# A convolution-style attention block and a token attention with top-2 experts on one core: a third of the copies into the query/key stacks moved from SyncE's queue to ScalarE's

## The reference

```
x   = x + proj(attention(group_norm(x)))            # conv block: 8 heads of 32, no mask
t   = tokens(x)                                      # 1024 tokens of 256
t   = t + W_O(causal_attention(layer_norm(t)))       # 8 heads of 32, causal
t   = t + experts(layer_norm(t))                     # 32 experts of 64, the 2 best by sigmoid gate
```

## Time and profile before

| | us |
|---|---|
| median of 3 runs | 3707.65 |
| the 3 runs | 3701.99 to 3708.15 |
| the profiled execution | 3706.1 |
| its span, first to last instruction | 3704.2 |
| PE busy | 3250.2 (88%) |
| DVE busy | 1999.4 (54%) |
| ACT busy | 1623.6 (44%) |
| POOL busy | 733.6 (20%) |

### The profile page before, as it was taken

One profiled execution on the slowest core, in us unless ns is written; L12 is line 12 of the kernel. 1 busy time (PEld: TensorE's weight loads), 2 busy tenths in 40 slices (PEclk: granted clock), 3 DMA queues, 4 the chain that ended last, 5 costly groups with the idle time before them and its releaser, 6 DMA issues.

```text
span 3704.2 us, 50690 instructions
## 1 busy us (share of the span) xinstructions
PE 3250.2 (88%) x19118; PEld 1846.8 (50%) x19118; DVE 1999.4 (54%) x2718; ACT 1623.6 (44%) x2423; POOL 733.6 (20%) x806
## 2 busy tenths in 40 slices
PE   3797989999898988989889898999989899898987
PEld 2334554465545555355544555446554465545555
DVE  5745366355754557445674546736466445753541
ACT  1271535435264442734437353453535435264442
POOL 0000031130301213022220303104031130302236
PEclk8596989899898998989989999989989999998999
DMA  4002040232303232041410505023240332304234
GB/s 114 0 18 63 19 131 24 77 112 64 103 7 106 83 93 74 22 124 49 126 47 18 148 24 143 29 64 108 58 115 18 86 103 70 98 7 124 65 93 125
DMA packets 155390, 273.38 MB, mean 74 GB/s; under 512 B 27024, under 2 KB 29072, under 8 KB 155024
## 3 DMA queue, kind: packets, MB, share of 16 engines
q1 hardware_dynamic: 155152, 270.16, 26.6%
HBM read 153.14 MB, written 10.49 MB: 44 GB/s over the span
## 4 chain that ended last, share of the span: by engine, by line
PE 62%; DVE 17%; issue 6%; ACT 5%; SPq 5%; DMA 4%; POOL 1%; DVEq 0%; ACTq 0%; POOLq 0%
PE ps_two L805 11%; DVE tops L1175 11%; PE ps_acc L677 10%; PE ps_acc L689 7%; PE ps_one L624 6%; PE ps_two L769 5%; PE ps_one L625 5%; PE ps_one L626 5%; SPq L530 4%; DMA probs<-gates_dram 3%; PE ps_acc L624 2%; ACT probs L976 2%; PE ps_one L710 2%; PE ps_acc L626 2%; PE ps_acc L625 2%
## 5 line engine op out<-in xcount | busy, mean ns | idle before, releaser
L1175 DVE TENSOR_REDUCE tops<-ps_two 128x2 bf16<-128x1024 f32 (+3 forms) x896 | 957.3, 1110 | 171.9 <-PE ps_two L769 122.1
L976 ACT ACTIVATE probs<-ps_two 128x1024 f32<-128x1024 f32 (+3 forms) x896 | 787.4, 929 | 261.2 <-PE ps_two L805 137.6
L595 POOL TENSOR_TENSOR nat<-probs,nat 128x256 fp32r<-128x256 f32 x512 | 374.4, 733 | 1860.9 <-ACT nat L911 1500.7
L805 PE MATMUL ps_two<-stacks 128*128 128x512 f32 (+3 forms) x1792 | 566.2, 419 | 19.8 <-ACT probs L976 12.6
L769 PE MATMUL ps_two<-stacks 32*128 32x512 f32 (+3 forms) x1792 | 441.1, 515 | 156.3 <-DVE tops L1175 136.8
L805 PEld LDWEIGHTS ps_two<-stacks 128*128 128x128 f32 x1792 | 308.7, 191 | 339.9 <-issue 183.2
L677 PE MATMUL ps_acc<-probs,v_sb 128*32 128x512 f32 (+3 forms) x3584 | 436.2, 559 | 0.0
L911 ACT CAST nat<-probs 128x256 fp32r<-128x256 f32 x256 | 103.6, 405 | 739.0 <-DVE probs L1298 547.6
L769 PEld LDWEIGHTS ps_two<-stacks 32*128 32x128 f32 x1792 | 179.1, 205 | 411.9 <-DVE tops L1175 210.7
L1298 DVE SCALAR_TENSOR_TENSOR probs<-ps_one,probs 128x512 f32<-128x512 f32 x256 | 176.6, 690 | 328.4 <-DMA probs<-gates_dram 152.9
L689 PE MATMUL ps_acc<-probs,ones 128*32 128x512 f32 (+3 forms) x2944 | 342.5, 537 | 0.0
(11 more groups left out here) (146 smaller groups left out, 4414.3 us busy)
## 6 DMA issues: line engine op xcount, KB each, us to landing
stacks<-nat SPq DMA_DIRECT2D x780, 128.0 KB, 2.4
probs<-experts_dram SPq DMA_DIRECT2D x256, 256.0 KB, 2.9
probs<-gates_dram SPq DMA_DIRECT2D x512, 128.0 KB, 3.0
x_in<-x_in_dram SPq DMA_DIRECT2D x9, 1024.0 KB, 5.0
xt<-x_res SPq DMA_DIRECT2D x8, 512.0 KB, 3.4
out_dram<-x_res SPq DMA_DIRECT2D x8, 512.0 KB, 2.8
out_dram<-xt SPq DMA_DIRECT2D x8, 512.0 KB, 3.1
w_hi<-w_image SPq DMA_DIRECT2D x7, 512.0 KB, 4.5
```

What stands on the lines that cost most here:

```text
L595: pool.tensor_tensor(parts[:, 1, j % 2, :], expert_sb[:, j % RING, c:c + C], f(parts[:, 0, j % 2, :]), ALU.subtract).then_inc(lowered, 1)
L805: mm = pe.matmul(at[:, a:HALF], k_st[0:P, g, j, P * k:P * k + P], q_st[0:P, g, j, HALF * hf + a:HALF * hf + HALF], start=True, stop=not diag)
L976: done(act.activation(probs[:, n % 2, per * i:per * i + per, a:HALF], acc[:, :, a:HALF], ACT.Exp, scale=SCALE), s + (i,))
L1175: done(dve.reduce_max(tops[:, kh, 2 * pr:2 * pr + 2, i], acc[:, :, 0:cols(st, i, kh)], AX_X), s)
```

## The change

The `stack` step of SP issues for each head only the first two of its three transfers. ScalarE, which did nothing in this step, now waits for the same three things as SP (both banks of q and k read by VectorE, and the `acc_read` count that says the old stacks are no longer used) and then issues the third transfer of each of the four heads, into partitions 64 to 95. Bytes, sources, destinations and the counts on `stacked` are the same.

```diff
@@ SP's stack step
                         for j in range(G):
                             rows = slice(HD * j, HD * j + HD)
-                            for quad, pair in enumerate(stacked_pairs(j)):
+                            for quad, pair in enumerate(stacked_pairs(j)[:2]):
                                 sp.dma_start(f(stacks[HD * quad:HD * quad + HD, :, g, j, half(hf)]),
                                              f(nat[rows, pair, half(hf)])).then_inc(stacked[g][hf][j], 16)
@@ ScalarE
+                    elif kind == "stack":
+                        _, st, g, hf = s
+                        read(("qk", st, g, "q", hf))
+                        read(("qk", st, g, "k", hf))
+                        if st:
+                            act.wait_ge(acc_read, sec.value("acc", sec.no["acc"][("norm", 0, g, NH - 1)]))
+                        elif g == 0 and hf == 0 and sec.name != "first":
+                            act.wait_ge(acc_read, sec.value("acc", sec.no["acc"][("norm", 1, 0, NH - 1)]))
+                        elif sec.name == "body":
+                            act.wait_ge(acc_read, sec.value("acc", 0))
+                        for j in range(G):
+                            act.dma_start(f(stacks[HD * 2:HD * 3, :, g, j, half(hf)]),
+                                          f(nat[HD * j:HD * j + HD, stacked_pairs(j)[2], half(hf)])).then_inc(stacked[g][hf][j], 16)
```

## The result

The changed kernel takes 3797.39 us in the median (4 runs, 3791.04 to 3809.59), against 3704.83 for the kernel before beside it (4 runs, 3701.99 to 3708.15): a ratio of 1.0253, 95% interval 1.0224 to 1.0283. The profiled execution took 3793.86 us, 87.8 more than the one of before; its span is 3792.1. The sign was forecast, the size was not: +93 us instead of +21, and outside the forecast's range of 3688 to 3770 us.

What follows compares the result with a forecast made beforehand. TensorE held 62% of the chain, VectorE 17%, SP's issuing 5%. Seven bodies at +3.0 us make 21, `first` and `head` -2, the last S8 +1.9: sum +21, 3728 us; range 3688 to 3770 us.

Steps and rivals of the forecast that it cites:

- S4: Stack step S4: ScalarE's next exponentials come late, TensorE needs their banks; cost 1.3 us a body (0 to 2.1).
- S5: Stack step S5: L999 ends late, VectorE and then TensorE wait for it; cost 1.5 us a body (0 to 4).
- S7: Stack step S7: ScalarE's copy of v frees its bank late for TensorE; cost 1.0 us a body (0 to 3.5).
- S8: Stack step S8: late exponentials against no more wait for the landing, between gain 0.5 and cost 1.9; +0.7 us a body.
- `first` and `head`: Parts outside the seven bodies: three waits on the landing at -2 us each, their S4 and S5 +4 together; sum -2.
- ScalarE pays: At each step ScalarE's queue issues four transfers at 0.64 us, standing for 2.57 us from VectorE's last lower part.
- SP gives back: At each of 65 steps SP issues 8 instead of 12, 2.57 us less, and its transfers still land last.
- S2: Stack step S2: landing 2.57 us earlier, projection 1.4 us later through the late root; gain 1.3 us a body.
- A rule beside the rows: Side-by-side copies assumed against the skill's shared-engines rule; by that rule S2 and S3 gain near nothing, sum about +35.
- The rival of full DMA engines: Rival, 15%: 0.9 busy is the engines' limit, only 0.8 of the 2.57 us is gained; +43, 3751 us.
- the clock as a term: TensorE's clock: shorter idle at S2 may gain about 1 us a body, new idle at S8 may take as much.
- S1: Stack step S1: `fin` is 3.7 us late, mostly hidden by TensorE's matmuls of v; +0.5 us a body (0 to 2).

Runs made afterwards that it cites:

- The runs with the order changed: Changed kernel with ScalarE's four transfers in head order 3, 2, 1, 0, or 2, 3, 0, 1: 3754.68 us (1.0124) and 3753.08 us (1.0097).
- the reversed order: Changed kernel with ScalarE's four transfers in head order 3, 2, 1, 0, SP still 0, 1, 2, 3: 3754.68 us, ratio 1.0124.
- the deferred kernel: Changed kernel with ScalarE's step moved later in its own queue at S1, S4, S5 and S7: 3757.83 us, ratio 1.0148.

## Why the prediction was wrong, point by point

- **What bounds the kernel, who waits at which place.** Right. The places where TensorE and VectorE wait now are the forecast ones, S4, S5, S7 and S8, S6 costs nothing, and ScalarE's wait for VectorE alone (1.09 us) is free. One reading was off by one: in `first` and `head` the chain passes through SP at four places, the fourth at 448 us.
- **"ScalarE pays", four issues at 0.64 us.** Undersized: 3.30 us instead of 2.57 for the four. ScalarE's queue alone does keep 0.65 us each; beside SP's it does not. The runs with the order changed go with 48 to 58 us less for these 0.74 us, some 20 of them apart from the clock.
- **"SP gives back" 2.57 us, the landing of SP's last unchanged.** This step failed: it took for granted that with two queues each transfer still lands 2.4 us after its issue, so that fewer issues on SP mean an earlier last landing. SP's issuing shrank by 1.57 us (7.72 to 6.15) and the last landing came 0.40 us earlier (9.66 to 9.26). With the third left out it came 2.64 us earlier, and the kernel was 73 us faster. So the gain at S2 was 0.0 instead of 1.3: ScalarE's idle ahead of L944 did shrink from 5.14 to 2.96 us at one S3, but its start was no earlier, 11.41 us after VectorE's lower part against 11.43. The root came 2.2 us late instead of the forecast 1.4, VectorE's work and the projection behind it as late, and the landing, hardly earlier than before, met them. In `first` and `head` together +12.5 instead of -2, of which 5.1 are the clock. Of the 67 us that the profiled growth lies above the forecast, S8 has 22, S7 20, `first` and `head` 14.5, S4 13 and S2 9, and the drift behind S3 takes 15 back.
- **"A rule beside the rows."** I saw 0.89 to 0.91 of the DMA engines busy at 199 to 204 GB/s, held the 382 of another shape against it and let the two queues run side by side. That row was no evidence of room: it had 128 partitions, these have 32. The Trainium skill's rule, "DMA: Bandwidth & Descriptors", section "Issuing engines are not separate DMA queues", is borne out by the traces as far as it says that a second issuing engine does not speed the transfers up (last landing 9.26 us against 9.66); they disagree with "usually small", since an issue takes 0.6 us and a transfer is finished every 0.66. I had priced it at +35. The rival of full DMA engines had the right mechanism at 15%, and was itself too low at +43, since it kept ScalarE's stop at 2.57 us.
- **S8, +0.7 forecast, +3.8 measured.** 2.0 of the 3.8 us are time at the lower clock, 1.8 are not. The slack was read on the wrong engine (and 3.7 less 1.57 is 2.1, not 1.9). ScalarE had been idle for 1.57 us before the second exponentials, but it waited for TensorE, and TensorE waits in turn for the first pair before it can go on: any delay of that pair over the time of the `mix` matmuls between is TensorE's idle. Even with half the rows and a stop of 2.46 us S8 costs 1.9. The gain that I set against it, no more wait of 2.38 us for the landing, did come (L944 starts at once), but it is paid for by the exponentials.
- **S7, +1.0 forecast, +3.8 measured.** What the forecast summed up was right: apart from the clock S7 costs under 1 us a body. The other 3.2 are time at the lower clock in the 120 us behind it. In that body the granted clock of the part from 1730 us on, where it fell to the lower level for 6.8 us at 1742, some 43 us behind the gap of 1.66 us, and of the same work in the kernel before:

```profile
1730.00:1760.00 30.00, 28.18 (x167) 16.51 (x165) 14.06 (x17) 10.01 (x16) 5.89 (x6) 0.89 0.17 58
```

```profile
1690.00:1720.00 30.00, 28.18 (x184) 16.35 (x186) 15.08 (x18) 10.82 (x17) 6.54 (x7) 1.00 0.18 62
```

  0.11 of 30 us are 3.3 us. That the gap brings the lower clock on is not shown by one body; the deferred kernel, without the gap, has 1.0 us of it behind S7 instead of 3.2. The prediction had the clock as a term for S2 and S8, of either sign, and not for S7.
- **S4, S5, S1.** S4 +3.1 for 1.3: with the short stop of the reversed order it is 1.4, so what was missed is the longer stop and, for 1.0 us, time at the lower clock behind the new gap; S5 +1.7 for 1.5 and S1 +1.1 for 0.5, about right.
- **Turning points.** "If a landing takes over 4 us, I am wrong": the medians are 3.7 and 3.9, the longest 6.2 and 6.1. "ScalarE's idle before L943 at S3 some 2.5 us shorter" came true (2.2 us at one S3) and meant nothing, since the start behind it did not move.

## What to carry to other kernels

Before a second queue is added, find out whether the issuing or the movement limits. That both have one spacing, as here (0.64 and 0.66 us), doesn't tell: the half-size transfers also land one per issue behind SP's later issues, and one in 0.32 us where two queues issue. Two queues with transfers of half the size, beside two queues with full ones, did tell. Issuing costs the issuing engine its queue, so ask what stands behind it and put it behind what others wait for, or on an engine with nothing behind it; here that, with the order of heads reversed, turned +2.5% into -1.0%. Look at the granted clock of every run beside its time: a change of 20 us here was in some kernels the clock and nothing else. And read slack on the engine that sets the end, not on the one that is stopped.

## What the runs showed of the chip

- An issue of a queue takes about 0.6 us whatever its size (0.59 to 0.62 for 32x1x512, 32x2x256 and 32x2x512), on SP and on ScalarE alike, 0.53 on GpSimd. ScalarE computes next to nothing meanwhile: 5.8 of the 210.7 us of its issues in the changed kernel overlap with its computing.
- Transfers of 32 partitions by 2 by 512 land one in 0.66 us from one queue and one in 0.56 to 0.68 from two, by the partitions that they read. With two queues at this size every step of the changed kernel has issues of over 0.9 us on both, at the S8 shown 0.98 to 1.29; with half the bytes ScalarE's four stay at 2.5 us.
- Which queue is held back depends on the partitions the two read. Between the orders of heads the sum of both hardly changes (9.45, 9.29 and 9.28 us); when ScalarE reads one half only it is 8.12 or 10.48.
